# Two output banks in a normalised self-attention block, and key rotation over three chunks at once in a masked cross-attention block

## What is computed

```python
# layer 2, self attention (16 query heads, 4 key heads of 64, repeated 4 times)
z = rmsnorm(latents, s3)
q, k, v = z@wq, z@wk, z@wv
q, k = q*rsqrt(mean(q*q)+EPS), k*rsqrt(mean(k*k)+EPS)      # per head
attn = softmax(q @ k.T / 8)
latents = latents + (attn @ v).reshape(B, T, H*Dh) @ wo
# layer 3, cross attention (16 query heads, 4 key heads of 64, 375 keys)
h, kv = rmsnorm(x, ln1_w), rmsnorm(ctx, ln1_w)
q, k, v = h@Wq, kv@Wk, kv@Wv
q, k = q*cos_q + rotate_half(q)*sin_q, k*cos_k + rotate_half(k)*sin_k
x = x + softmax(q @ k.T / 8 + attention_mask) @ v @ Wo
```

## Time and profile before

| | us |
|---|---|
| median of 3 runs | 1947.57 |
| lowest, highest | 1942.87, 1950.38 |
| the profiled execution | 1943.69 |
| its span, first to last instruction | 1941.9 |
| TensorE busy in the span | 1740.7 |
| VectorE busy in the span | 1297.7 |
| ScalarE busy in the span | 842.2 |
| GpSimd busy in the span | 704.9 |

### The profile page before, as it was taken

One profiled execution on the slowest core, in us unless ns is written; L12 is line 12 of the kernel. 1 busy time (PEld: TensorE's weight loads), 2 busy tenths in 40 slices (PEclk: granted clock), 3 DMA queues, 4 the chain that ended last, 5 costly groups with the idle time before them and its releaser, 6 DMA issues.

```text
span 1941.9 us, 35088 instructions
## 1 busy us (share of the span) xinstructions
PE 1740.7 (90%) x11106; PEld 1239.9 (64%) x11106; DVE 1297.7 (67%) x3310; ACT 842.2 (43%) x2473; POOL 704.9 (36%) x796
## 2 busy tenths in 40 slices
PE   5979998889997879999799999998988989998998
PEld 4756665679986668666685455585545855565577
DVE  5866777511127886888765665897778967566665
ACT  3645555333334642656324444343233445444431
POOL 2325555230012234667332333340001445454543
PEclk9989999789998989999999999999999999999999
DMA  4100000288972000012100020101001000000200
GB/s 175 33 24 17 17 8 16 78 287 323 326 253 98 1 0 22 31 46 75 69 11 17 17 73 0 55 1 66 1 0 69 9 1 23 14 12 12 77 1 19
DMA packets 37015, 115.22 MB, mean 59 GB/s; under 512 B 3344, under 2 KB 23728, under 8 KB 29728
## 3 DMA queue, kind: packets, MB, share of 16 engines
q1 hardware_dynamic: 34352, 107.33, 15.8%
q0 software_dynamic: 2544, 6.43, 1.0%
HBM read 99.34 MB, written 14.40 MB: 59 GB/s over the span
## 4 chain that ended last, share of the span: by engine, by line
PE 55%; DVE 23%; issue 10%; POOL 5%; ACT 4%; DMA 1%; DVEq 1%; POOLq 0%; SPq 0%; ACTq 0%
PE ps L1060 7%; PE ps L1100 5%; PE ps L862 5%; PE ps L938 4%; PE ps L1210 4%; PE ps L1222 4%; PE ps L993 4%; POOL arena L2111 4%; PE ps L971 3%; PE ps L910 3%; PE ps L857 3%; PE ps L966 2%; DVE arena L1787 2%; PE ps L835 2%; PE ps L915 2%
## 5 line engine op out<-in xcount | busy, mean ns | idle before, releaser
L2111 POOL TENSOR_TENSOR arena<-arena,rinv 112x375 f32<-112x375 f32 (+1 forms) x448 | 370.8, 830 | 461.7 <-DVE rinv L1770 449.5
L938 PEld LDWEIGHTS ps<-cst,arena 112*125 112x125 f32 (+1 forms) x1408 | 186.5, 181 | 168.1 <-POOL arena L2111 83.7
L938 PE MATMUL ps<-cst,arena 112*125 112x112 f32 (+1 forms) x1408 | 245.0, 291 | 39.3 <-POOL arena L2111 35.8
L1343 ACT ACTIVATE arena<-ps,negmax 112x375 f32<-112x375 f32 (+1 forms) x384 | 190.6, 501 | 153.5 <-DVE negmax L1765 153.1
L1779 DVE COPY arena<-ps 125x336 f32<-125x336 f32 x384 | 190.4, 496 | 44.3 <-PE ps L938 43.4
L1765 DVE TENSOR_REDUCE negmax<-ps 112x1 f32<-112x375 f32 (+1 forms) x288 | 158.1, 549 | 64.7 <-PE ps L910 57.4
L1343 ACT ACTIVATE arena<-arena,negmax 112x112 f32<-112x112 f32 (+1 forms) x256 | 125.6, 491 | 143.3 <-DVE negmax L1754 96.5
L1060 PE MATMUL ps<-h_split_sb,w_split_sb 128*128 128x448 f32 x768 | 171.7, 370 | 6.9 <-POOL w_split_sb L2187 3.0
L1060 PEld LDWEIGHTS ps<-h_split_sb,w_split_sb 128*128 128x128 f32 x768 | 144.7, 190 | 23.5 <-POOL w_split_sb L2187 4.9
L857 PE MATMUL ps<-wat,arena 128*125 128x256 f32 (+1 forms) x576 | 142.7, 385 | 2.4 <-DVE arena L1673 1.5
L2187 POOL TENSOR_TENSOR w_split_sb<-wml,w_split_sb 128x512 fp32r<-128x512 f32 (+1 forms) x40 | 46.9, 1171 | 233.9 <-ACT w_split_sb L1409 232.0
(11 more groups left out here) (230 smaller groups left out, 3264.3 us busy)
## 6 DMA issues: line engine op xcount, KB each, us to landing
wml<-in_wm_L_moe SPq DMA_DIRECT2D x21, 1028.0 KB, 6.9
wml<-in_wm_L_moe SPq DMA_DIRECT2D x21, 1024.0 KB, 7.9
craw<-in_ctx SPq DMA_DIRECT2D x32, 375.0 KB
wml<-in_wm_L_m SPq DMA_DIRECT2D x3, 3072.0 KB, 14.3
wat<-in_wa_L_ca SPq DMA_DIRECT2D x2, 2560.0 KB, 9.3
wml<-in_wm_L_m SPq DMA_DIRECT2D x2, 2048.0 KB, 10.2
keys_hbm<-arena SPq DMA_DIRECT2D x8, 375.0 KB
arena<-keys_hbm SPq DMA_DIRECT2D x8, 375.0 KB
```

The lines of the kernel that those rows point to most:

```text
L938: last = nc.tensor.transpose(ps[0:blk.kp, T_BANK + s % blk.t_banks, o:o + S], buf[:, i * blk.nk + q * blk.kp:i * blk.nk + (q + 1) * blk.kp ...
L1343: last = go(probs[0:S, s % blk.nprobs, i * nk:(i + 1) * nk], src[:, i * nk:(i + 1) * nk], ACT.Exp, scale=-1.0 if blk.mask == "input" else ...
L2111: pool.tensor_tensor(p3, p3, r3, ALU.mult).then_inc(scaled, 1)
```

## The change

- L2_sa gets two banks for outputs (6 and 3, one for each half) and two for sums (4 and 5). `weigh` of each half waits for the divide of the same half of the batch before; `divide` waits for the multiply before it, as both use one buffer `inverse`.
- Banks 3 and 5 were the projection's and a piece's. The projection goes to bank 7, the pieces go round banks 7 and 2. V0 now shares bank 7 with the projection and is not an early piece, so it waits for the add of the projection (`out_done`), and it stands between QT0 and QT1 in the plan.
- KS is evacuated by ScalarE, times 8, into `var`, and VectorE scales queries' and keys' sums in one instruction instead of two. The projection waits for that evacuation, as KS is in bank 7.
- The last output of L2_m1 goes to bank 5, since no piece of L2_sa uses it any more. The warm-up transposes of QT0 come ahead of V0 in the first batch; those at the end of the block go to bank 2. L2_m2's second chunk doesn't wait for the last add, as `out_bank` is above the scores' banks.
- In L3_ca kr0, kr1 and kr2 issue one instruction each over all three chunks.

```diff
     "L2_sa": dict(
-        plan={0: ["XT"], 1: ["K0", "QP0", "QP1", "KS"], 3: ["V0", "QT0", "QT1"]},
+        plan={0: ["XT"], 1: ["K0", "QP0", "QP1", "KS"], 3: ["QT0", "V0", "QT1"]},
...
-        out_step=3, lag=2, s_banks=2, t_banks=2, w_banks=[7, 5, 2], out_bank=3),
+        out_step=3, lag=2, s_banks=2, t_banks=2, w_banks=[7, 2], out_bank=7, o_banks=(6, 3), l_banks=(4, 5)),
...
+        self.o_banks, self.l_banks = plan.get("o_banks", (6, 6)), plan.get("l_banks", (4, 4))
+        self.two_outs = "o_banks" in plan
...
                     if g == blk.wg - 1:
-                        wait(pe, o_done, count(st["o"], blk.no, b))
+                        wait(pe, o_done, count(st["o"], blk.no, b, -1 if blk.two_outs else 0))
...
                     if g == 3 and blk.no == 2:
-                        pe.wait_ge(o_done, count(st["o"], blk.no, b, 1))
+                        pe.wait_ge(o_done, count(st["o"], blk.no, b, 0 if blk.two_outs else 1))
...
-                                last = mm(ps[64 * z:64 * z + 64, O_BANK, 0:HG * S], vz64[0:kp, par, q, (g - 1 + z) * 64:(g + z) * 64],
+                                last = mm(ps[64 * z:64 * z + 64, blk.o_banks[g // 2], 0:HG * S], vz64[0:kp, par, q, (g - 1 + z) * 64:(g + z) * 64],
...
-                            last = mm(ps[64 * z:64 * z + 64, L_BANK, 0:HG * S], ones[0:kp], sums, start=True, stop=True,
+                            last = mm(ps[64 * z:64 * z + 64, blk.l_banks[g // 2], 0:HG * S], ones[0:kp], sums, start=True, stop=True,
...
-                    if name == "Q" and not blk.cross or name == "KS":
+                    if name == "Q" and not blk.cross:
                         return
...
+                    elif name == "KS":
+                        last = go(var[0:kp, H:H + 4 * blk.kc], W[0:kp, 0:4 * blk.kc], ACT.Copy, scale=8.0)
...
                         if blk.key_scale:
-                            W = ps[0:kp, blk.w_banks[blk.bank_of["KS"]], 0:4 * blk.kc]
-                            link(v.tensor_scalar(var[0:S, 0:H], var[0:S, 0:H], 1.0 / 64, blk.eps, ALU.mult, ALU.add))
-                            dve.wait_ge(w_full, count(st["w"], np_, m, blk.pieces.index("KS") + 1))
-                            v.tensor_scalar(var[0:kp, H:k], W, 8.0 / 64, blk.eps, ALU.mult, ALU.add).then_inc(w_done[blk.bank_of["KS"]], 1)
                             dve.wait_ge(*evacuated(blk, st, m, "KS"))
-                        else:
-                            link(v.tensor_scalar(var[0:kp, 0:k], var[0:kp, 0:k], 1.0 / 64, blk.eps, ALU.mult, ALU.add))
+                        link(v.tensor_scalar(var[0:kp, 0:k], var[0:kp, 0:k], 1.0 / 64, blk.eps, ALU.mult, ALU.add))
...
-                        for q in range(KC):
-                            cos = cs("cosk", KC * 64, KP)[:, q * 64:(q + 1) * 64].unsqueeze(1)
-                            sin = cs("sink", KC * 64, KP)[:, q * 64:(q + 1) * 64].unsqueeze(1)
-                            if name == "kr0":
-                                if q == 0:
-                                    dve.wait_ge(*evacuated(blk, st, m, "KP1"))
-                                last = v.tensor_tensor(s4[:, q, :, 0:32], k4[:, q, :, 32:64], sin[:, :, 0:32].broadcast_to([KP, 4, 32]), ALU.mult)
...
+                        cos, sin = (cs(x, KC * 64, KP).rearrange("p (k d) -> p k d", k=KC).unsqueeze(2) for x in ("cosk", "sink"))
+                        if name == "kr0":
+                            dve.wait_ge(*evacuated(blk, st, m, "KP1"))
+                            last = v.tensor_tensor(s4[:, :, :, 0:32], k4[:, :, :, 32:64], sin[:, :, :, 0:32].broadcast_to([KP, KC, 4, 32]), ALU.mult)
+                        elif name == "kr1":
+                            last = v.tensor_tensor(s4[:, :, :, 32:64], k4[:, :, :, 0:32], sin[:, :, :, 32:64].broadcast_to([KP, KC, 4, 32]), ALU.mult)
+                        elif name == "kr2":
+                            last = v.tensor_tensor(k4, k4, cos.broadcast_to([KP, KC, 4, 64]), ALU.mult)
...
                     dve.wait_ge(av_done, count(st["group"], 2, b, p + 1))
-                    v.reciprocal(inverse, ps[:, L_BANK, 0:HG * S]).then_inc(inverted, 1)
+                    if blk.two_outs:
+                        wait(dve, o_done, count(st["o"], 2, b, p))
+                    v.reciprocal(inverse, ps[:, blk.l_banks[p], 0:HG * S]).then_inc(inverted, 1)
                     dve.wait_ge(inverted, count(st["pair"], 2, b, p + 1))
-                    v.tensor_tensor(oT[:, 4 * p:4 * p + 4], ps[:, O_BANK, 0:HG * S].rearrange("p (r s) -> p r s", s=S),
+                    v.tensor_tensor(oT[:, 4 * p:4 * p + 4], ps[:, blk.o_banks[p], 0:HG * S].rearrange("p (r s) -> p r s", s=S),
```

More of the change, by code:

```diff
@@ L1725, in extra @@
                         s4 = sq[0:KP, 0:KC * D].rearrange("p (k h d) -> p k h d", k=KC, d=64)
-                        for q in range(KC):
-                            cos = cs("cosk", KC * 64, KP)[:, q * 64:(q + 1) * 64].unsqueeze(1)
-                            sin = cs("sink", KC * 64, KP)[:, q * 64:(q + 1) * 64].unsqueeze(1)
-                            if name == "kr0":
-                                if q == 0:
-                                    dve.wait_ge(*evacuated(blk, st, m, "KP1"))
-                                last = v.tensor_tensor(s4[:, q, :, 0:32], k4[:, q, :, 32:64], sin[:, :, 0:32].broadcast_to([KP, 4, 32]), ALU.mult)
-                            elif name == "kr1":
-                                last = v.tensor_tensor(s4[:, q, :, 32:64], k4[:, q, :, 0:32], sin[:, :, 32:64].broadcast_to([KP, 4, 32]), ALU.mult)
-                            elif name == "kr2":
-                                last = v.tensor_tensor(k4[:, q], k4[:, q], cos.broadcast_to([KP, 4, 64]), ALU.mult)
+                        cos, sin = (cs(x, KC * 64, KP).rearrange("p (k d) -> p k d", k=KC).unsqueeze(2) for x in ("cosk", "sink"))
[6 more added lines that the diff above has]
+                            last = v.tensor_tensor(k4, k4, cos.broadcast_to([KP, KC, 4, 64]), ALU.mult)
                         if name == "kr3":
```

## The result

The changed kernel takes 1917.78 us (median of 4 runs, 1914.93 to 1919.13) against 1948.97 us for the kernel before (4 runs, 1942.87 to 1952.12): a ratio of 0.984, 95% interval 0.9816 to 0.9864. In the profiled executions the span went from 1941.9 to 1913.1 us, 28.8 us less. Laid side by side, matmul by matmul, the two traces part in two places: over the self block 10.2 us are gained from its first matmul to the first one behind it, 10.7 with the wait just ahead of it that the forecast counts (forecast 10.3), and over the masked cross block 20.7 us (forecast 7.7). All lines of the code have moved: the scaling L1705 is now L1704, the divide L1787 and L1789 is L1785 and L1787, L971 is L973, L1779 is L1775, L1732 to L1738 are L1728 to L1734, L820 is L822, L1576 is L1580.

What follows compares the result with a forecast made beforehand. The prediction took TensorE, busy 90% of the span, as the bound, so only its waits counted. 10.3 us (self block) + 7.7 (rotation) = 18.0 us off 1943.69 gave 1925.7, or 1929.6 for the median; range 1921 to 1939.

Steps and rivals of the forecast that it cites:

- the sum's 10.3 us: Self block: gain from separate banks, ScalarE's key sums, steadier clock and block edges; 10.3 us, between 5 and 12.5.
- a ring of 16.7: Self block: after the change one batch, closed through TensorE and VectorE, takes 16.7 us instead of 17.96.
- the row at 1485.24: End of the self block: VectorE's own wait of 1.03 us goes; 1.0 us gained (0 to 2.0).
- rival 1: Self block: the clock falls all the same, 3.2 us are missing, 1932.8 us; chance 0.15.
- rival 3: Self block: V0 waits behind the projection's add and takes back 1.08 us a batch; 1937.9 us, chance 0.07.
- The key sums: Self block: ScalarE's copy of KS takes 0.2 us a batch off VectorE's chain; at most 0.2 lost if late.
- Rival 4's ring: Self block: L971, divide, key squares, KS, ScalarE's copy, projection, add, V0; 14.1 us, slower kernel if delayed: 1962, chance 0.04.
- The rotation: Masked cross block: merging nine instructions into three gains 1.1 us a batch, seven times: 7.7 us (2.1 to 9.4).
- following both engines: Masked cross block: VectorE and GpSimd traced through the second rotation step give about 0.45 us more, 1.4 together.
- Rival 2: Masked cross block: merging saves only its fixed cost, 2.1 instead of 7.7 us; 1935.2 us, chance 0.12.
- the cross block's account: Masked cross block: TensorE waits 9.1 us in 8 waits at L971 for VectorE's copies at L1779.
- Theory D: From the experiments: VectorE's instructions come in 8192-byte packets; a loop body crossing one boundary more is fetched anew each pass.

Runs made afterwards that it cites:

- rot_only: Kernel before with only kr0 to kr2 merged into one instruction each, self block as before: 1928.03 us, ratio 0.9891.
- before_shift: Kernel before with 88 dead memsets at VectorE's start, moving the masked cross block's loop 87 places later: 1939.03 us, ratio 0.9958.
- ks_dve: Changed kernel with the key sums read from PSUM by VectorE again, no copy by ScalarE: 1929.83 us, ratio 0.9907.
- pad_inner: Changed kernel with three dead memsets on VectorE ahead of each of kr0, kr1 and kr2, in the loop alone: 1930.06 us, ratio 0.9908.

## Why the prediction was wrong

**The self block was right, and as near as that by luck.** Of the sum's 10.3 us, 10.2 to 10.7 came. Other traces with this part of the change give 8.4 to 11.3, and in rot_only and before_shift, whose self block is that of the kernel before, the block is 1.7 and 1.5 us longer than in the trace before: there the second and third distances between scalings are 19.1 to 19.6 us, where that trace has 17.37 and 18.02. Nor did the terms come out one by one: the repeating batches gained more than 1.28 us each (16.4 us, where a ring of 16.7 was forecast), since the transposes start 1.28 us behind the scaling and not 1.41, and from them to L973 are 3.06 us (1407.84 to 1410.90), not 3.23. The first batch lost 1.4 instead of 1.1. At the block's end the row at 1485.24 lost its wait, but 3.8 us of waiting at L995 came up; behind the block's last scaling 0.5 us were gained of the 1.0. Both falls of the clock in the middle are gone, so rival 1 is refuted, and rival 3 with it: V0 does not wait.

**The key sums were right as a term and misread as a part.** The step costed the copy as 0.2 us off VectorE's chain, and from L971 to the next scaling 0.19 us did go (12.24 to 12.05). Its larger worth is that it frees the projection's bank early, and without it the block gains nothing (ks_dve). The sum came out right because the change has both; where the key sums are read late, TensorE stands 2.4 us at a time and the scalings lie 1.8 to 3.6 us further apart, where the step had "at most 0.2". Rival 4's ring goes through this copy; the place was right, its price stayed at 0.17 us.

**The rotation was near in size, by luck, and wrong in its split.** 7.7 us were forecast; the changed kernel's 20.7 less the 11.0 of before_shift leave 9.7, and rot_only's 18.8 and the 18.5 of the changed kernel's second trace leave 7.8 and 7.5. The split was wrong: 0.95 us a batch for the first step and 0.45 for the second, where 1.4 / 7 = 0.2 and 5.7 / 7 = 0.8 were measured. The step "following both engines" followed VectorE and GpSimd past each other, and left out that VectorE's next instruction behind the first step has to wait for TensorE. It had GpSimd's multiply ahead of the second step; in the changed kernel VectorE is 0.06 us ahead of it, and in pad_inner, where the multiply is ahead, the step saves 0.09 us and not 0.45. Of the up to 0.55 us that GpSimd was to stand behind a merged step, 0.35 are seen at the second (1.44 against 1.09). Rival 2, the fixed cost alone, is refuted. The third step, "saves nothing", became longer: 9.8 us in 7 instructions, 1.40 us a batch, where 24 took 8.7 us in 8 batches, 1.09 a batch.

**The step that failed** is the cross block's account of what TensorE waits for. It took in the 8 waits for L1779 and left out the 5.6 us at L820 (2.68 and 2.92), which stand in the same view: they were put at nothing, without a word. With the low clock behind them, moving the loop was worth 11.0 us of the cross block in before_shift, and 9.7 us of the kernel's time. No term and no rival held it. The gains as read are 10.2 (self block) + 11.0 (place of the loop) + 9.7 (what is left of the cross block, for the rotation) = 30.9 us; 2.5 us had been lost ahead of the self block and 0.4 were gained elsewhere, which leaves the 28.8 of the spans. And "nine instructions become three" was priced by their durations alone, while it also shifted the end of the loop from 2892 to 2874.

What runs do not show is how the store of instructions works. The traces show packets of 8192 bytes on q14, ten fewer where the edges are free, and a limit for the body's end between 2882 and 2892 that comes back free at 2979 with a start of 2659. The Trainium skill (Runtime: NRT & Kernel Launch, "Instruction fetch mechanics") says that most engines hold two blocks of 256 instructions, filled in the order of the program, and that a branch back to a block that is no longer held waits for a fetch. The trace agrees with the kind of event, at 2.4 to 3.5 us a branch with two packets starting about it, and with the gain of a move by 87 places; the Trainium skill's blocks are 16 KiB where the packets here are 8 KiB. By the figures of that page of the Trainium skill, as an estimate, a body of 320 has to begin within the first 192 of 256 places; no run here tests that width. Theory D's packets, with three of them held, fit every run as well. This rule bears on a change that alters the number of instructions, and the prediction did not weigh it.

## What to carry to other kernels

In a loop, look at each engine's first instruction behind the back edge: idle there that ends in "issue", with instruction packets starting there, is a fetch ("issue" alone is not enough: the changed kernel shows 1.04 us of it at 1589.67, with no packet in it), and a few dead instructions in an early idle stretch can be worth more than a saved step (88 memsets: 0.4%). When a change adds or takes away instructions, ask where each later loop then lies in the engine's program, for the result can hang on that (18 memsets outside the loop: 8.1 us back in that block). And price a changed evacuation by who needs the bank next, not by the instruction saved.

## What was not expected of the hardware

- A loop of 308 instructions on VectorE runs over its back edge without idle at 2566 to 2874 and stands 3.12 and 3.07 us at 2584 to 2892; one of 320 stands 3.07 and 3.30 us at 2572 to 2892 and is free at 2659 to 2979.
- Such an edge costs more than its idle: the two, 6.4 us of VectorE's idle and 5.6 us of TensorE's, were worth 9.8 us. The granted clock behind them was 0.66, and 0.52 and 0.80; with the loop moved it is 1.00 there.
- A VectorE multiply that starts 0.06 us ahead of GpSimd's runs at its own 0.55 us and lengthens GpSimd's from 1.09 to 1.44; one that starts 0.01 us behind takes 1.49 and leaves GpSimd's at 1.09; the same work in three instructions took 1.58.
